# A fused convolution, Mamba and attention kernel: attention scores as fp32 products in four row tiles of TensorE instead of bf16 products of split operands

## The reference, cut to what matters

```
q = w_q @ x1 ; k = w_k @ x1          # (32, 4096) each
v = w_v @ x1                         # (64, 4096)
energy_s = q.T @ k                   # (4096, 4096)
attn_s = softmax(energy_s, axis=-1)
out_s = v @ attn_s.T                 # (64, 4096)
out = x1 + w_bn @ concat([channel_attention(x1), out_s])
```

## Time and profile before

| | us |
|---|---|
| median of 3 runs | 8543.9 (8539.67 to 8546.88) |
| the profiled execution | 8545.51 |
| its span, first to last instruction | 8543.7 |
| TensorE busy | 7863.7 (92%) |
| VectorE busy | 6747.1 (79%) |
| ScalarE busy | 5998.1 (70%) |
| GpSimd busy | 3411.3 (40%) |

### The profile page before, as it was taken

How to read it: one execution, slowest core, us unless ns; L and a number is a source line. 1 busy time by engine, 2 the same in 40 slices (tenths; PEclk the granted TensorE clock), 3 DMA queues, 4 the chain that set the end, 5 groups by cost and what they waited for, 6 DMA issues and landing times. The chain is left out here.

```text
span 8543.7 us, 138038 instructions
## 1 busy us (share of the span) xinstructions
PE 7863.7 (92%) x39494; PEld 2293.2 (27%) x39494; DVE 6747.1 (79%) x10982; ACT 5998.1 (70%) x10582; POOL 3411.3 (40%) x4135
## 2 busy tenths in 40 slices
PE   8972489999999999999999999999999999999999
PEld 2220122222222222222222222222222222222222
DVE  2228888888888888888888898888888888888721
ACT  1114577777878778777778787777877787877754
POOL 0006544444444444444444444444444444444300
PEclk9986589999999999999999999999999999999999
DMA  8748877777787777777777878777777878777500
GB/s 130 119 87 218 221 193 196 201 189 195 186 202 194 195 193 200 190 184 197 195 202 185 203 193 195 194 182 195 197 197 194 204 186 202 194 182 197 142 23 11
DMA packets 868062, 1530.20 MB, mean 179 GB/s; under 512 B 403336, under 2 KB 436944, under 8 KB 867280
## 3 DMA queue, kind: packets, MB, share of 16 engines
q1 hardware_dynamic: 864208, 1520.77, 72.7%
q10 hardware_dynamic: 3072, 0.40, 0.0%
HBM read 1326.69 MB, written 176.95 MB: 176 GB/s over the span
## 5 line engine op out<-in xcount | busy, mean ns | idle before, releaser
L1260 POOL TENSOR_TENSOR hst<-hst,cbc 128x512 f32<-128x512 f32 x2048 | 2611.4, 1275 | 3724.4 <-DVE bank L1132 3702.5
L1143 DVE TENSOR_TENSOR_SCAN hst<-dA,carry,bank 128x512 f32<-128x512 f32 x1792 | 2293.8, 1280 | 161.2 <-DVE bank L1132 60.8
L998 ACT ACTIVATE pr<-bank 128x512 f32<-128x512 f32 x4096 | 2223.4, 601 | 61.7 <-PE bank L894 59.4
L903 PE MATMUL bank<-pr,vt 128*64 128x512 f32 x8192 | 2220.6, 621 | 0.0
L943 ACT ACTIVATE gains<-bank 128x512 f32<-128x512 f32 x2048 | 1224.9, 598 | 1253.5 <-PE bank L834 963.7
L892 PE MATMUL bank<-s1q,s1k 128*128 128x512 bf16 x4096 | 1562.7, 382 | 171.7 <-ACT pr L998 152.3
L834 PE MATMUL bank<-s1kx,s1q 128*128 128x512 bf16 x4096 | 1584.5, 388 | 124.1 <-DMA s1kx<-kx_d 45.2
L1004 ACT ACTIVATE dA<-lanes,small 128x512 f32<-128x512 f32 x2048 | 1502.7, 734 | 210.7 <-DMA lanes<-spread_d 172.2
L1084 DVE CUSTOM_DVE_ANT_0 gains<-bank,gains 128x512 f32<-128x512 f32 x2048 | 1369.6, 669 | 332.9 <-PE bank L834 325.0
L1132 DVE TENSOR_TENSOR bank<-lanes,bbc 128x512 f32<-128x512 f32 x2048 | 1514.2, 739 | 106.8 <-DMA lanes<-spread_d 42.0
L894 PE MATMUL bank<-t2q,t2k 128*128 128x512 bf16 x4096 | 1560.2, 381 | 0.0
(11 more groups left out here) (116 smaller groups left out, 5815.4 us busy)
## 6 DMA issues: line engine op xcount, KB each, us to landing
lanes<-spread_d SPq DMA_DIRECT2D x2048, 512.0 KB, 5.7
seqt<-seq_d SPq DMA_DIRECT2D x256, 128.0 KB, 4.5
spread_d<-dsp SPq DMA_DIRECT2D x128, 256.0 KB, 2.0
spread_d<-usp SPq DMA_DIRECT2D x128, 256.0 KB, 2.0
bbc<-bc_d SPq DMA_DIRECT2D x128, 256.0 KB, 3.5
cbc<-bc_d SPq DMA_DIRECT2D x128, 256.0 KB, 4.1
xpad<-in_x SPq DMA_DIRECT2D x64, 256.0 KB, 6.8
ypad<-ypad SPq DMA_DIRECT2D x128, 128.0 KB, 4.2
```

The lines of the kernel that those rows point to most:

```text
L903: mm = nc.tensor.matmul(ACC[CH * h:CH * (h + 1), :], vt[:, t, :], pr[:, T % PRING, h, :], start=t == 0, stop=t == KT - 1)
L998: nc.scalar.activation(pr[:, T % PRING, h, :], bank_of(("S", T, h))[:], ACT.Exp).then_inc(S["p_full"], 1)
L1143: nc.vector.tensor_tensor_scan(hst[:, slot_of(T), :], dA[:, T % 2, :], DBU[:], carry[:, g:g + 1] if sl % CHUNKS else 0.0, ALU.mult, ALU.ad ...
L1260: nc.gpsimd.tensor_tensor(h, h, cbc[:, (T - 1) // GROUPS % 2, :], ALU.mult).then_inc(S["hc_in"], 1)
```

## The change

Queries and keys stay fp32 with 32 rows (`QDIM`). The array is used as four row tiles of 32 rows. Copies of the keys and queries lie at rows 0 and 32 (for S0 and S1), the key difference at 64 (dif) and the second key at 96 (max). All four products of a tick are issued side by side. Then two bf16 products of three rows each, `shifts`, add the negated maxima to the scores. `plan` now takes the banks in the order dif, max, S0, S1, and all four bank waits (`ready`) stand ahead of the first of the four products. The casts, subtractions and three of the five stores are gone, and the loads are fewer. The maxima's row is issued as six DMAs instead of three.

```diff
-QUERY_PARTS, KEY_PARTS = (0, 1, 0, 1), (1, 0, 0, 1)
+ROW_S0, ROW_S1, ROW_DIF, ROW_MAX = (QDIM * r for r in range(4))
...
-        plan = [e for e in uses if e[0] == "dif"]
+        plan = [e for e in uses if e[0] in ("dif", "max")]
         if self.attends(T):
             plan += [("S", T, 0), ("S", T, 1)]
-        plan += [e for e in uses if e[0] == "max"]
...
-                                for part, t in enumerate((head, mid, low)):
-                                    issued(sp.dma_start(into[:, part, :, cols], t[CH:P, 0:CHUNK]), "st_split")
-                                for part, t in enumerate((head, mid)):
-                                    issued(sp.dma_start(kx_d[...], t[CH + QDIM:P, HALF:WIDE]), "st_split")
+                                issued(sp.dma_start(image_of(qk_d, a)[:, cols], x1c[CH:P, c % 2, 0:CHUNK]), "st_split")
+                                issued(sp.dma_start(image_of(kd_d, a)[:, k * HALF:(k + 1) * HALF],
+                                                    x1c[CH + QDIM:P, c % 2, CHUNK:WIDE]), "st_split")
...
+                            o = ROW_DIF if kind == "dif" else ROW_MAX
+                            mm = nc.tensor.matmul(bank[:], query[o:o + QDIM, q, nt * P:(nt + 1) * P],
+                                                  keys[o:o + QDIM, mc * CHUNK:(mc + 1) * CHUNK],
+                                                  start=True, stop=True, tile_position=(o, 0))
...
-                        nc.tensor.matmul(bank[:], s1k[:, t * P:(t + 1) * P], s1q[:, q, cols],
-                                         start=True, stop=False)
-                        nc.tensor.matmul(bank[:], t2k[:, t * P:(t + 1) * P], t2q[:, q, cols],
-                                         start=False, stop=True).then_inc(S["ring_full"], 1)
+                        o = ROW_S1 if h else ROW_S0
+                        nc.tensor.matmul(bank_of(e)[:], keys[o:o + QDIM, t * P:(t + 1) * P],
+                                         query[o:o + QDIM, q, 0:CHUNK], start=True, stop=False, tile_position=(o, 0))
+
+                    def shifts(e):
+                        T, h = e[1:]
+                        (a, q), o = sched.attends(T), ROW_S1 if h else ROW_S0
+                        nc.tensor.matmul(bank_of(e)[:], one3[o:o + 3, :], nmq[o:o + 3, q, :], start=False, stop=True,
+                                         tile_position=(o, 0)).then_inc(S["ring_full"], 1)
...
+                        group = [e for e in plan if e[0] in ("dif", "max", "S")]
+                        for e in group:
+                            ready(e)
+                        for e in group:
                             if e[0] == "S":
                                 scores(e)
-                            elif e[0] == "PV":
+                            else:
+                                small_use(e)
+                        for e in group:
+                            if e[0] == "S":
+                                shifts(e)
+                        for e in plan[len(group):]:
+                            if e[0] == "PV":
...
                             for s in range(3):
-                                act.dma_start(t2q[CH + s:CH + s + 1, q, :], nm3[:, s, :]).then_inc(S["nm_row"], 16)
+                                for h, o in enumerate((ROW_S0, ROW_S1)):
+                                    act.dma_start(nmq[o + s:o + s + 1, q, :],
+                                                  nm3[4 * h:4 * (h + 1), s, :]).then_inc(S["nm_row"], 16)
...
-                        if sched.chunk(c) and r == 9:
-                            nc.scalar.copy(head[CH:P, :], x1c[CH:P, c % 2, :]).then_inc(S["head_in"], 1)
-                        if sched.chunk(c) and r == 11:
-                            nc.scalar.copy(mid[CH:P, :], rest[CH:P, :]).then_inc(S["mid_in"], 1)
...
-                            nc.vector.tensor_tensor(rest[CH:P, :], x1c[CH:P, c % 2, :], head[CH:P, :],
-                                                    ALU.subtract).then_inc(S["rest_in"], 1)
-                            nc.vector.tensor_tensor(low[CH:P, :], rest[CH:P, 0:CHUNK], mid[CH:P, 0:CHUNK],
-                                                    ALU.subtract).then_inc(S["low_in"], 1)
```

More of the change, by code:

```diff
@@ L464, in pipeline @@
         x1c = sb("x1c", [P, 2, WIDE])
[L465 to L469, removed]
+        bcs = sb("bcs", [2 * D_STATE, CHUNK])
         gains = sb("gains", [P, 2, CHUNK])
@@ L668, in issued, with load_search @@
                         total[name] = total.get(name, 0) + 16
[L670 to L680, removed]
+                    def load_search(a, p, name):
+                        half = slice(p * CHUNK, (p + 1) * CHUNK)
+                        issued(sp.dma_start(keys[ROW_DIF:ROW_DIF + QDIM, half], image_of(kd_d, a)[:, half]), name)
+                        second = image_of(qk_d, a)[QDIM:CH].rearrange("p (c h n) -> p c h n", h=2, n=HALF)
+                        issued(sp.dma_start(keys[ROW_MAX:ROW_MAX + QDIM, half].rearrange("p (c n) -> p c n", n=HALF),
+                                            second[:, 2 * p:2 * (p + 1), 1, :]), name)
                     if first < 0:
@@ L807, in _ @@
                                                     accs[CH * h:CH * (h + 1), :]), "st_out")
-                    total["nm_row"] = 48 * len(sched.counts.get("nm_row", ()))
+                    total["nm_row"] = 96 * len(sched.counts.get("nm_row", ()))
                     for name, value in total.items():
@@ L825, in small_use @@
                         kind, c = e[0], e[1]
-                        bank = take_bank(e)
+                        bank = bank_of(e) if kind in ("dif", "max") else take_bank(e)
                         if kind in ("dif", "max"):
@@ L829, in small_use @@
                             nt, mc = k % NT, k // NT
-                            if k == 0:
-                                wait(pe, f"ld_q{q}", (a, q), 16 * 6)
-                            if q == 0 and k % NT == 0:
-                                wait(pe, f"ld_kx{mc}", a, 16 * 4)
-                            mm = nc.tensor.matmul(bank[:].rearrange("p (c n) -> p c n", n=HALF),
-                                                  s1q[:, q, nt * P:(nt + 1) * P],
-                                                  keys[:, 2 * mc:2 * (mc + 1), 1 if kind == "dif" else 0, :],
-                                                  start=True, stop=True)
+                            o = ROW_DIF if kind == "dif" else ROW_MAX
+                            mm = nc.tensor.matmul(bank[:], query[o:o + QDIM, q, nt * P:(nt + 1) * P],
+                                                  keys[o:o + QDIM, mc * CHUNK:(mc + 1) * CHUNK],
+                                                  start=True, stop=True, tile_position=(o, 0))
                         elif kind == "turn":
@@ L881, in small_use, with ready @@
                         mm.then_inc(S["ring_full"], 1)
+                    def ready(e):
+                        kind = e[0]
+                        take_bank(e)
+                        if kind == "S":
+                            T = e[1]
+                            (a, q), t = sched.attends(T), (T - MAIN) % KT
+                            if t == 0:
+                                wait(pe, "nm_row", (a, q), 96)
+                            if q == 0 and t % 8 == 0:
+                                wait(pe, f"ld_k{t // 8}", a, 16 * 3)
+                        elif kind == "dif":
+                            (a, q), k = e[1:]
+                            if k == 0:
+                                wait(pe, f"ld_q{q}", (a, q), 16 * 4)
+                            if q == 0 and k % NT == 0:
+                                wait(pe, f"ld_kx{k // NT}", a, 16 * 2)
                     def scores(e):
@@ L963, in small_use @@
                             taken(act, ("xv", c - 2))
-                            wait(act, "rest_in", c - 2)
+                            wait(act, "kd_in", c - 2)
+                            wait(act, "st_split", c - 2, 32)
                         elif kind == "xv":
@@ L977, in small_use @@
                         elif kind == "BC":
-                            dst, src = bcs, bank[0:2 * D_STATE, :]
+                            dst, src = bcs[:], bank[0:2 * D_STATE, :]
                         elif kind == "out":
@@ L1091, in small_use @@
                         elif kind == "turn":
-                            wait(dve, "nm_row", sched.before(c), 48)
+                            wait(dve, "nm_row", sched.before(c), 96)
                             nc.vector.tensor_scalar(nmx[:, 0, :], bank[0:NT, 0:P], -1.0, None,
```

88 lines of the change are left out of this document (32 added, 56 removed).

## The result

The changed kernel takes 9404.2 us (median of five, 9400.4 to 9415.3) against 8540.8 for the kernel before in the same measurement: ratio 1.101, 95% interval 1.0996 to 1.1026. It is slower, as forecast, but by 863 us where 398 were forecast, and it lies just above the range's end of 9400. The profiled execution took 9403.4, with a span of 9401.5.

A forecast was written before the change was run, and what follows sets the result against it. TensorE was taken as the bound, VectorE close behind. Per chunk 53.9 us own work + 5.6 gate waits + 3.0 DMAs + 0.1 turn = 62.6, its neighbour 60.1; mean +3.5 over 118 chunks gave 8942 us, range 8700 to 9150 (80%: 8640 to 9400).

The forecast's parts named there:

- The group's own time: TensorE per tick: four fp32 products 0.96 us plus 0.31 to PV, put at 1.28 with issue, against 1.40 before.
- weight loads that queue: Loads of tiles 3 and 4 come one by one: group 0.37 us longer in 12 ticks, 9460 us; chance 0.12.
- two tiles at a time: Four products take two rounds, 0.86 us more per TensorE-paced tick: 10150 us; chance 0.06.
- the estimate of 1.57: Group time if four row tiles give 3.07 times: four products 1.25 us, group 1.57, about 9370 us.
- The gate: All four banks awaited before a tick's first product: waits at r = 3, 5, 9, 15, 0 and others, 5.6 us per chunk.
- ScalarE's DMAs: Six issues instead of three at r = 12 of every second chunk: 1.0 to 3.0 us, 3.0 taken.
- The step that failed: TensorE's products after a stop kept their usual times: 1.27 us for the group, 1.01 for PV.
- The sum: Chunks of 62.6 and 60.1 us, mean +3.5; 118 chunks +413, the rest -15: 8942 us median.
- rival 1: Waits for banks cost nothing, only TensorE's 1.9 us per chunk saved counts: 8315 us; chance 0.14.
- The rival that the gate costs nothing: Same as rival 1: ScalarE and VectorE done when TensorE returns, waits under 1.9 us per chunk plus DMAs; chance 0.14.

The follow-up runs named there:

- e1: Kernel before, bf16 products kept, with only the change's bank order and its gate (four bank waits ahead of the first product): 9078.8 us, 1.063.
- e3: Changed kernel plus unread fp32 products in TensorE's two long stops, four at r = 10, six after the DMA stop: 9147.9 us, 1.0712.
- e5: Kernel before with only its three DMAs of the maxima's row split into six half-row ones: 8721.7 us, 1.0202.
- e2: Changed kernel with the six DMAs of the maxima's row issued by SyncE a tick later, instead of by ScalarE: 9188.4 us, 1.0754.
- e9: Changed kernel with bank order dif, S0, S1, max, each fp32 product waiting only for its own bank: 9120.3 us, 1.067.
- e8: Changed kernel, maxima's DMAs from SyncE, bank order dif, S0, S1, max, six-bank ring, VectorE's lanes-times-B product in SBUF: 8955.3 us, 1.0479.

## Why the prediction was right in direction and short in size

- **The group's own time: right.** 1.28 said, 1.29 measured. Both rivals on row tiles, weight loads that queue and two tiles at a time, are out, and so is the estimate of 1.57 by the Trainium skill's factor 3.07 ("TensorE: Matmul & The Clock Gate", "Measured speedup vs the span model"): here four tiles of 32 rows cost what two of 64 do.
- **The gate: right in place and nearly in size.** e1 shows it alone: 540 us. With the clock kept up (e3) the chunk is 63.82 us where the forecast's is 61.4. Of the 2.4 missing, 0.9 are in the kernel before as well (58.79 measured, 57.86 reckoned from one chunk and its neighbour). The rest, 1.5 per chunk or some 177 us: r = 7 by 0.44, r = 3 by 0.24 (0.26 us lay between the max's end and the next product, 0.05 were assumed), r = 9 by 0.17, r = 11 by 0.15, and smaller ones. Why r = 7 rose stays open.
- **ScalarE's DMAs: right.** An issue of half the rows costs as much as a whole one (e5); the upper bound was the value to take. e2 gives 216 us back, half clock included; 3.0 us in some 60 quarters were 180.
- **The step that failed: each wait was priced at its idle time.** The prediction took 0.96 and 1.01 us for products behind a stop of 2 or 3 us, as for all others. It looked at the stops of 1.30 and 0.24 us, behind which nothing is slow, and named no bound for longer ones. The price stood in the trace of before: between 2000 and 8000 us ten of its twelve stops of 1.75 to 3.25 us were followed by half clock. One of them, where TensorE waits for a load of keys:

```profile
3418.27 0.38 PE L834 MATMUL bank<-s1kx,s1q 128*128 128x512 bf16 x1 [2.63 <-DMA s1kx<-kx_d]
...
3420.38 1.98 PE L903 MATMUL bank<-pr,vt 128*64 128x512 f32 x4
3422.29 1.06 PE L917 MATMUL bank<-pr,ones 128*32 128x512 f32 x8
```

  The group takes 2.11 us there instead of 1.40 and PV 1.91 instead of 1.01, 1.6 us more together. The change makes a stop of 2.2 us in each chunk and one of 2.9 in every second. At 1.6 us each that would have been up to some 280 us, an estimate from these rows. e3 measured what comes behind the stops: 256 us.
- **The sum.** 398 forecast + 256 for the clock + 177 for the waits = 831 of 863; 32 are open. (A slip that changes nothing: rival 1's 8544 - 118 x 1.9 is 8320, not 8315.)
- **The rival that the gate costs nothing** is out by e1. Its condition, waits under 1.9 us per chunk, was missed by far.

## What to carry to other kernels

Before waits are gathered ahead of a group that is to run side by side, ask for the last bank of the group which engine frees it and when; here a ring that let the busiest engine run one tick ahead was worth 540 us (e1), the shorter products 0.1 us per tick. Price a stop twice: its idle time, and the products behind it, at half clock, if it grows longer than the stops that the trace of before shows at full clock (here from 1.3 us to over 2). Search the trace of before for stops of the new length, even if they are rare: they show the price. A small DMA is not small for the queue that issues it.

## What the runs showed of the hardware

- Four fp32 products in row tiles of 32 rows, into four banks, start within 0.02 us of each other and last 1.14 us together; one product on the whole array lasts 1.12.
- Half clock (granted 0.55 in a window of 3.83 us) came after none of the stops of 1.25 to 1.75 us in the five profiles of the table, and after 211 of the 294 from 1.75 to 3.25 us. In e9, with one row tile by itself ahead of the stop, it came after 41 of 41 of 1.25 to 1.75 us.
- Unread products in the two long stops kept the clock (0.99 between 3000 and 7000 us instead of 0.96) and made the kernel 2.7% faster (e3).
- A DMA issue from ScalarE's queue takes about the same for 1 KB (0.61 and 0.63 us, six in 3.65 and 3.76) and for 2 KB (0.66, three in 1.97).
- With VectorE's product of lanes and B in SBUF instead of PSUM (e8), GpSimd's product of the same size took 2072 ns instead of 1276 and VectorE's scan 1453 instead of 1280.
